# A new front, a batched shared expert and six folds inside the first routed stretch of a macaron block

## The reference

```python
router_logits = x @ gate_w                       # 16 experts
scores = sigmoid(router_logits)
_, selected = top_k(scores + expert_bias, 2)
top_scores = scores[selected] / (sum + 1e-20)
shared = silu(x @ shared_gate_w) * (x @ shared_up_w) @ shared_down_w
for e in range(E):                               # F = 128
    g, u = split(x @ experts_gate_up[e])
    routed += comb[:, e:e+1] * (silu(g) * u @ experts_down[e])
ffn = shared + routed

Q, K, V = x Wq^T, x Wk^T, x Wv^T                 # 3 heads of 256
attn = mean over heads of softmax(Q K^T / 16, over the query axis) V
out = attn @ fc_w.T + fc_b
```

## Time and profile before

| | us |
|---|---|
| median of 3 runs | 603.43 |
| lowest and highest | 601.87, 606.74 |
| the profiled execution | 605.9 |
| its span, first to last instruction | 604.7 |

### The profile page before, as it was taken

How to read it: one execution, slowest core, us unless ns; L and a number is a source line. 1 busy time by engine, 2 the same in 40 slices (tenths; PEclk the granted TensorE clock), 3 DMA queues, 4 the chain that set the end, 5 groups by cost and what they waited for, 6 DMA issues and landing times.

```text
span 604.7 us, 10587 instructions
## 1 busy us (share of the span) xinstructions
PE 478.6 (79%) x3212; PEld 434.0 (72%) x3212; DVE 366.6 (61%) x1118; ACT 274.9 (45%) x771; POOL 270.1 (45%) x278
## 2 busy tenths in 40 slices
PE   3632389999886799799899988999675899999600
PEld 3632389999774598699879977999563799998500
DVE  5567477566566366557645865543637776766543
ACT  3451147677541444354435443456241277776200
POOL 4654536566042163255226522422203566660675
PEclk9999999999998899899989999999955599999755
DMA  8661134667762010011001100010110156677455
GB/s 277 202 210 34 53 106 150 180 189 147 177 199 70 5 48 2 0 36 54 18 1 41 48 19 2 0 36 1 36 61 10 34 149 177 184 164 177 125 159 142
DMA packets 41077, 56.29 MB, mean 93 GB/s; under 512 B 6272, under 2 KB 33792, under 8 KB 41024
## 3 DMA queue, kind: packets, MB, share of 16 engines
q1 hardware_dynamic: 33024, 34.88, 17.8%
q0 software_dynamic: 7584, 20.72, 15.0%
q10 hardware_dynamic: 416, 0.02, 0.0%
HBM read 36.99 MB, written 18.61 MB: 92 GB/s over the span
## 4 chain that ended last, share of the span: by engine, by line
PE 59%; DVE 14%; DMA 12%; issue 5%; ACT 5%; POOL 5%; SPq 0%; POOLq 0%; ACTq 0%; DVEq 0%
PE bank L299 47%; PE bank L305 6%; DMA stage<-y_dram,slot_i 5%; DMA raw<-xn_dram,gather_at 2%; PE bank L432 2%; DMA raw<-xn_dram 2%; DVE x_sb L991 1%; PE bank L334 1%; POOL stage L1217 1%; DVE softmax_row L1114 1%; POOL w_lo L1167 1%; PE bank L389 1%; DVE x_sb L957 1%; DVE xn L817 1%; DMA xn_dram<-xn 1%
## 5 line engine op out<-in xcount | busy, mean ns | idle before, releaser
L299 PE MATMUL bank<-w_hi,xT 128*128 (+1 forms) x504 | 128.6, 317 | 0.0
L1323 POOL TENSOR_TENSOR e_sp<-raw,e_sp 128x512 fp32r<-128x512 f32 x48 | 62.5, 1302 | 134.7 <-ACT e_sp L773 134.6
L1246 POOL DMA_INDIRECT raw<-xn_dram,gather_at x94 | 89.3, 950 | 57.7 <-PE bank L305 46.8
L299 PEld LDWEIGHTS bank<-w_hi,xT 128*128 128x128 f32 x504 | 92.7, 202 | 0.3
L1217 POOL DMA_INDIRECT stage<-y_dram,slot_i x64 | 61.2, 957 | 51.8 <-issue 26.4
L299 PEld LDWEIGHTS bank<-v_sp,e_sp 128*128 128x128 f32 x576 | 75.8, 194 | 4.0 <-POOL e_sp L1323 1.1
L299 PE MATMUL bank<-v_sp,e_sp 128*128 128x256 f32 x576 | 78.0, 286 | 0.9 <-POOL e_sp L1323 0.9
L299 PE MATMUL bank<-g_sp,xT 128*128 128x512 f32 x288 | 75.2, 396 | 1.4 <-DVE g_sp L1022 1.4
L299 PE MATMUL bank<-w_lo,xT 128*128 (+1 forms) x252 | 74.2, 294 | 0.0
L299 PE MATMUL bank<-w_hi,e_sp 128*128 (+1 forms) x252 | 71.3, 303 | 2.0 <-DVE x_sb L1015 1.8
L305 PE MATMUL bank<-ident,raw 128*128 128x128 f32 x292 | 62.4, 298 | 8.8 <-DMA raw<-xn_dram 5.5
(11 more groups left out here) (112 smaller groups left out, 892.1 us busy)
## 6 DMA issues: line engine op xcount, KB each, us to landing
y_dram<-stage SPq DMA_DIRECT2D x94, 128.0 KB
raw<-xn_dram SPq DMA_DIRECT2D x32, 128.0 KB, 2.3
stage<-in_w_pack SPq DMA_DIRECT2D x9, 384.0 KB, 3.5
raw<-in_w_pack SPq DMA_DIRECT2D x8, 384.0 KB, 3.7
xn_dram<-raw SPq DMA_DIRECT2D x20, 128.0 KB, 1.7
x_sb<-in_x SPq DMA_DIRECT2D x4, 512.0 KB, 5.6
out<-x_sb SPq DMA_DIRECT2D x16, 128.0 KB, 2.3
raw<-xn_dram,gather_at POOLq DMA_INDIRECT x94, 3.4
```

What stands on the lines that cost most here:

```text
L299: m = pe.matmul(dst, lhs[k][l], rhs[k][r], start=(first and k == 0 and i == 0), stop=(last and k == n - 1 and i == 2), skip_group_check=True)
L1246: pool.indirect_dma_start(row_buf[:, n % ROWS, :], None, xn_dram, bass.IndirectOffsetOnAxis(ap=gather_at[:, j:j + 1], axis=0)).then_inc(s_ ...
L1323: pool.tensor_tensor(e_sp[:, i, 1, :], e32[:, i, :], e_sp[:, i, 0, :].bitcast(F32), ALU.subtract).then_inc(s_e_lo, 1)
```

## The change

**Front.** `STAGES` becomes 6. x is normalised by ScalarE into `xn_all`, which holds all 16 tiles; the scale and shift come from three small POOL instructions and a power. Tiles are turned in pairs into one bank, split into two parts for all 512 tokens of a batch (`front_x`), and the router uses three passes with a split gate. A whole batch is stored with one DMA. `xn_all` and a part of `front_x` lie where the folded weights lie later, and the new weight buffers where `e_sp` and `v_sp` lie.

**Shared expert.** It is taken out of the stretch, whose loop now has only the 47 slot tiles. It is made per batch: gate and up with 12 matmuls of 512 tokens (`shared_gu`), silu, product and two parts at 512 wide, and `shared_y` with 12 matmuls of 256. In the first FFN batches 0 to 2 are made beside the routing and batch 3 behind the stretch; in the second all four are made beside the routing.

**Index.** The picks are made in four chunks of eight pairs with no ring: one lane instruction a pair, and two wide instructions for all the tiles of a chunk.

**Folds.** All six are made in the first stretch, at steps 6, 13, 20, 27, 34 and 41 (`FOLD_STEPS`).

**Second front.** The normalised rows of batches 0 to 2, made beside attention and stored, are loaded back (`reload_batch`) and turned again; two pairs are turned ahead of attention's last mix.

```diff
-    EARLY = 8
-    STAGES = 4
-    FOLD_EVERY = 24
-    items = ([(SHARED, t) for t in range(EARLY)] + [(SLOT, j) for j in range(SLOT_TILES)]
-             + [(SHARED, t) for t in range(EARLY, NT)])
-    NI = len(items)
+    CHUNK = 8
+    EARLY_SHARED = 3
+    STAGES = 6
+    FOLD_STEPS = (6, 13, 20, 27, 34, 41)
+    NI = SLOT_TILES
...
@@ TensorE
+            def front_turn(r, n):
...
+                if n >= 2:
+                    pe.wait_ge(s_pair_lo, r * FRONT_PAIRS + n - 1)
...
+                for q in range(2):
+                    for k in range(KH):
+                        m = pe.transpose(bank[n % 2][:, k * PAIR + q * P:k * PAIR + (q + 1) * P],
+                                         xn_all[:, 2 * n + q, k * P:(k + 1) * P], ident[:])
+            def shared_gu(r, b):
...
+                for half, done in ((0, s_sg), (1, s_su)):
...
+                    three_pass(bank[shared_banks(b)[half]][:], lhs, rhs).then_inc(done, 1)
+            def shared_y(r, b):
+                pe.wait_ge(s_slo, c + 1)
...
+                    m = three_pass(bank[q // 2][:, q % 2 * H:(q % 2 + 1) * H],
+                                   [[shared_hT[:, part, q * P:(q + 1) * P] for part in range(2)]],
+                                   [[w_hi[:, at:at + H], w_lo[:, at:at + H]]])
...
+            for n in range(FRONT_PAIRS + 1):
+                if n < FRONT_PAIRS:
+                    front_turn(0, n)
+                if n > 0:
+                    front_router(0, n - 1)
+            shared_gu(0, 0)
+            shared_gu(0, 1)
+            rank_tokens(0)
+            shared_y(0, 0)
+            shared_gu(0, 2)
+            pack_experts(0)
+            shared_y(0, 1)
+            index_tokens(0)
+            shared_y(0, 2)
+            def between1(s):
+                if s in FOLD_STEPS:
+                    fold(next(folded))
+            ffn(0, between1)
+            shared_gu(0, 3)
+            shared_y(0, 3)
...
+            for w in MIXED_LATER:
+                if w == U - 1:
+                    front_turn(1, 0)
+                    front_turn(1, 1)
                 mix(w)
+            for n in range(2, FRONT_PAIRS - BATCH_PAIRS):
+                front_turn(1, n)
+            shared_gu(1, 0)
+            shared_gu(1, 1)
+            for n in range(FRONT_PAIRS - BATCH_PAIRS, FRONT_PAIRS):
+                front_turn(1, n)
+            for n in range(FRONT_PAIRS - BATCH_PAIRS, FRONT_PAIRS):
+                front_router(1, n)
+            rank_tokens(1)
+            shared_y(1, 0)
+            shared_gu(1, 2)
+            pack_experts(1)
+            shared_y(1, 1)
+            shared_gu(1, 3)
+            index_tokens(1)
+            shared_y(1, 2)
+            shared_y(1, 3)
+            ffn(1, lambda s: None)
...
@@ ScalarE, first front
+            front_norm(0, 0)
+            front_norm(0, 1)
+            front_hi(0, 0)
+            split_weight(0)
+            front_hi(0, 1)
+            front_norm(0, 2)
+            front_hi(0, 2)
+            split_weight(1)
...
+            run(choose(0, 0, NT))
+            shared_silu(0, 0)
+            shared_silu(0, 1)
+            for n in range(4, 8):
+                split_weight(n)
+            shared_hi(0, 0)
+            for n in range(8, 11):
+                split_weight(n)
+            shared_silu(0, 2)
+            shared_hi(0, 1)
+            for n in range(11, 14):
+                split_weight(n)
+            shared_hi(0, 2)
+            for n in range(14, NW):
+                split_weight(n)
...
@@ VectorE, the picks in routing
+                for c in range(len(pairs_of) // CHUNK):
+                    for n in range(c * CHUNK, (c + 1) * CHUNK):
+                        if n % 4 != 1:
+                            dve.tensor_scalar(pick_lane[:, n, :], lane_no[:], lane_i[:, k, t:t + 1], None,
+                                              ALU.is_equal).then_inc(s_lane_dve, 1)
...
+                    chained(dve.tensor_tensor(
...
+                    dve.tensor_tensor(pick_tile[:, t0:t1], pick_tile[:, t0:t1],
+                                      token_no[:, t0:t1].unsqueeze(2).unsqueeze(3).to_broadcast(shape),
+                                      ALU.mult).then_inc(s_pick_tile, 1)
...
-                dve.wait_ge(s_inv, (r + 1) * len(pairs_of))
+                dve.wait_ge(s_inv, r + 1)
                 dve.tensor_copy(gather_at[:], index).then_inc(s_indexed, 1)
...
@@ VectorE, first front after choose
+            shared_mul(0, 0)
+            shared_mul(0, 1)
+            r1 = routing(0)
+            next(r1)
+            next(r1)
+            shared_lo(0, 0)
+            next(r1)
+            next(r1)
+            next(r1)
+            split_weight(5)
+            next(r1)
+            shared_sink(0, 0)
+            shared_mul(0, 2)
+            next(r1)
+            shared_lo(0, 1)
+            next(r1)
+            split_weight(8)
+            next(r1)
+            shared_sink(0, 1)
+            split_weight(11)
+            shared_lo(0, 2)
+            split_weight(14)
+            shared_sink(0, 2)
+            run(r1)
...
@@ VectorE, second front after choose
+            shared_mul(1, 0)
+            shared_mul(1, 1)
+            r2 = routing(1)
...
+            shared_lo(1, 0)
...
+            shared_sink(1, 0)
+            shared_mul(1, 2)
+            shared_lo(1, 1)
...
+            shared_sink(1, 1)
+            next(r2)
+            shared_mul(1, 3)
+            shared_lo(1, 2)
+            shared_sink(1, 2)
+            shared_lo(1, 3)
+            shared_sink(1, 3)
+            run(r2)
...
@@ POOL, first front
+            for b in range(B):
+                front_rstd(0, b)
+            for n in range(NW):
+                if n % 3 != 2:
+                    split_weight(n)
+                    if n == 12:
+                        lanes(0)
...
@@ SP, first front
             for n in range(STAGES):
                 load_weight(n)
+            for b in range(B):
+                store_batch(0, b)
+            for n in range(STAGES, NW):
+                load_weight(n)
+            load_fold(0)
```

More of the change, by code:

```diff
@@ L186, in macaron @@
         fcb_sb = route[:, 6, 0:H]
-        stages = [buf[:, i * WCOLS:(i + 1) * WCOLS] for buf in (stage, raw) for i in range(2)]
+        stages = [buf[:, i * WCOLS:(i + 1) * WCOLS] for buf in (stage, raw, stage_more) for i in range(2)]
         fold_in = route[:, 0:4, :].rearrange("p (m k) h -> p m k h", m=2)
@@ L728, in act_program @@
-            next(r1)
-            splits = iter(range(NW))
-            for n in range(50):
-                if NW * (n + 1) // 50 > NW * n // 50:
-                    split_weight(next(splits))
-                next(r1)
-            attn_side = [attn_front(b) for b in range(B)]
+            act.wait_ge(s_zeroed, 1)
+            act.activation(score[:, 0, 0:1], minus_half[:, 0:1], ACT.Sigmoid).then_inc(s_warm, 1)
+            act.wait_ge(s_small, 32)
+            act.copy(gate_sp[:, 0], gate_raw[:]).then_inc(s_gate_hi, 1)
@@ L749, in act_program @@
+            shared_hi(0, 3)
+            attn_side = [attn_front(b) for b in range(B)]
             run(attn_side[0])
@@ L1379, in choose @@
                 for _ in range(4 + 2 * (n // 4)):
-                    yield
-            def routing():
-                for _ in range(4 + len(pairs_of) // GROUP + 1 + 2):
                     yield
```

863 lines of the change are left out of this document (409 added, 454 removed).

## The result

The changed kernel took 615.7 us (median of four runs, 614.8 to 616.7), the kernel before, run beside it, 604.0: ratio 1.019, 95% interval 1.015 to 1.024. It is slower. The forecast was 605, no change, with 599 to 611 as its own range; 615.7 lies outside that and inside the whole range of 588 to 618, near its slow end. The profiled execution's span (first to last instruction) is 615.1 us, where it was 604.7.

What follows compares the result with a forecast made beforehand. Routing, weights and index were taken to bound the first front, TensorE the first routed stretch. Terms -16.0 + 2.5 + 11.2 - 3.2 + 5.5 + 1.5 = +1.5 gave 605 us, no change; range 588 to 618, its own 599 to 611.

Steps and rivals of the forecast that it cites:

- the first front: Start to slot 0: the new order brings slot 0 to 71.8 instead of 87.8, -16.0 us (-22 to -10).
- the second rival: Both fronts: VectorE's chain bounds, POOL blocks in full, weights slide; +15, 618 us; chance 0.30 together with the third.
- the last three-pass router: First front, after ScalarE's last copy at 22.7: lower half and 12 small matmuls, done at 25.3.
- the GpSimd block: First front: POOL's weight splits hold up VectorE's counting, up to 7 us or nothing; 2.6 taken.
- Folds and fill: First routed stretch: four more folds at 2.8 us, +11.2, and filling the pipeline, +2.5 (1 to 4).
- Last product to attention: After the first stretch: the fold ahead of attention's turns is gone, -3.2 us (-1 to -5); shared batch 3 hidden.
- Second front: Before the second stretch: shared batches and sinks ahead of the index move slot 0 by +5.5 us (-1 to +11).
- rival 4: Both fronts: index ready early, copied late behind sinks; copied at once, 4 us each, 597; chance 0.34 with another rival.
- The granted clock: Second front: taken as 0.54; far over that was named as a sign of the prediction being wrong.
- Second stretch: Slot 0 to first result gather: filling costs +2.5, 1 comes back without shared rows loaded; +1.5 us (0 to 4).
- The third: First stretch: the folds' loads collide with gathers, 16 instead of 11.2, 610 us; chance 0.30 together with the second rival.

Runs made afterwards that it cites:

- stacked router: Changed kernel with early weight splits, early index copy and the first front's router products in 8 instead of 12 matmuls a pair: 603.1 us, on another chip 591.8 us.
- the kernel that only waits: Changed kernel with GpSimd's fourth low part of a weight waiting until VectorE has counted, all else the same: 626.1 us, ratio 1.004.

## Where the prediction held and where it failed, step by step

The result lies in the stated range, but not by the mechanism of the forecast: the first front failed by 16.1 us, and smaller errors of the other sign, 8 us together, brought the sum back within 11. The range reached to 618 for the sake of the second rival; that 615.7 fell inside it was partly luck.

**The first front, -16.0 and in fact +0.1: this is the step that failed,** and with it the forecast. Its own working gives two errors, which the runs confirm one by one.

1. "ScalarE has ... 1.7 us, eight pairs 13.6, last copy at 22.7", then "the last three-pass router": the router's matmuls were counted for the last pair alone, as if TensorE did the others beside ScalarE's work. They are TensorE's own pace: 12 matmuls at 0.215, which is 2.6, and the turns make 3.33 a pair in steady state. 8 x (3.33 - 1.7) is 13.0 of the 13.5 us by which the router was late (38.8 against 25.3). With one product instead of three a pair took 1.6 to 2.4 us, 1.9 in the mean, and the router ended at 27.5. Forgetting them cost so much because TensorE stood at its low level: at the second front's 0.119 a matmul and 8 turns in 1.03 us, a pair would be some 1.9 us (an estimate from these rows), and the router late by 2. The price stood in the trace of the kernel before, whose first front has the same small matmuls:

```profile
12.06 0.87 PE L334 MATMUL bank<-gate_raw,route 128*128 128x16 f32 x4
```

2. "I take 2.6" for the GpSimd block: the upper bound of 7 was the right end. Count to the last step of the slots took 11.9 us in the changed kernel and 5.3 where GpSimd waited, 6.6 us. Three more instructions between 74.5 and 81.8 took 4.8 us more than their shapes do elsewhere (2.52, 2.29 and 2.57 against 0.95, 0.68 and 0.95), a second meeting that the prediction didn't have. The rest of the chain was some 3 us shorter than counted, so ranks to index was 35.8 us, not 27.8 and 2.6. The Trainium skill, SBUF — State Buffer, section "Who interferes with whom", has the shared port pair as an exclusive lock, for which a VectorE instruction with two SBUF inputs contends with a GpSimd instruction that reads SBUF. The trace agrees: 5.46 us against 0.80 for the same four additions. I had cited the rule and weighed it by one cast of 1.09 us, which had met GpSimd only in part.

Together they are the 16.3 us by which the index was late (82.9 for 66.6, the 64.0 and the 2.6 for the block): the router 13.5, less 2.6 for the shared batches and ranks behind it, which took 8.3 us where I had 10.9, and 5.4 for the chain (35.8 for 30.4). The index's way to slot 0 was 4.9 for 5.2.

**Folds and fill, +13.7 and in fact +9.8.** The fold was 2.56 for 2.8, its number right; four make 10.2. The fill cost +3.0 (slots 0 to 5 turned within 10.0 us, where five plain steps make 7.0), for 2.5. What I had not subtracted is that 51 plain steps at 1.40 and two folds made 77 us of the old 81.0: the old stretch held another 4 us, the new one 1.0 (90.8 less 71.4 of steps, 15.4 of folds and 3.0 of fill). The trace of the kernel before shows where most of it lay. From slot 42 on its turns lost 2.3 us to late rows, 1.33 of them in one wait:

```profile
161.55 0.44 PE L305 MATMUL bank<-ident,raw 128*128 128x128 f32 x2 [1.33 <-DMA raw<-xn_dram,gather_at]
```

And from the turn of the last slot to the last product it took 7.2 us, where the new stretch, which turns nothing more there, took 6.5. Why the rows were late was not tried.

**Last product to attention, -3.2 and in fact -3.3.** Right in size; the reason given, that the fold ahead of the turns is gone, fits the rows and was not tested alone. That shared batch 3 hides there holds too: taking it away brought attention 0.3 us nearer to the gather.

**Second front, +5.5 and in fact +3.9.** Ranks to index 26.8 us, in the 25 to 28 given. The index was late behind the sinks, as rival 4 said, but copying it at once is worth 2 to 4 us in this front, not 4 in each: in the first it is worth nothing, where the last low parts then release slot 0, and 1.6 once the weights are early. In the changed kernel itself the index did release slot 0, as said, but by 2 us only: the last low parts ended at 80.9 and 81.8. The granted clock was 0.83, not near 0.54. I had named that as a sign of being wrong; this front's term held all the same.

**Second stretch, +1.5 and in fact -1.0.** Outside its bounds of 0 to 4 by 1 us. The fill came, but smaller (slots 0 to 5 turned within 8.2 us, 1.2 over plain steps, for 2.5). The rest is again time of the old stretch over plain steps: there the last slot's turn to the first result gather took 11.2 us, here 9.4.

**The rivals.** The second one happened, by its own test: slot 0 after 76 in the first front and after 489 in the second. Its mechanism, the block in full with the weights sliding, is part of the failed term; it lacked the router. Its 618 is 2 us from the result, the forecast 11, but its terms are not the measured ones (first front -10 for +0.1, second front +10 for +3.9, its fill +3 for -1.0), so the nearness is luck. The third, loads of the folds colliding with gathers, 16 instead of 11.2, didn't happen: four folds cost 10.2, and with three of the six outside the stretch the time stayed at 616.7. With the router counted for every pair at 3.33 the sum would have been 605 + 13.0, and slower the likeliest case. That this is near 615.7 owes something to chance too: the 5.4 missing for the block and 8 us too much in the other terms would still have stood in it.

## What to carry to other kernels

A pipelined loop over tiles has a pace on each engine, so write down for each engine all that it does for one tile and take the largest; a term that stands in the sum "for the last one" is often the pace of all. Where two engines hold each other up, as VectorE and GpSimd did here (four additions 5.46 us beside the low parts, 0.80 without), ask which of one's long instructions will stand beside the other's short chained ones after a reordering. Put them where the other waits; here a wait alone only moved the bill. A block of fixed work (a fold) cost its time in the stretch, which TensorE paced, and as much behind it, where it waited for its own matrices; in a gap that another engine made it cost little (1 us at most for the fold at 53.5): look for the gap before choosing the step.

## What the runs showed of the hardware that was not expected

**The granted clock read 1.00 while TensorE's pace was that of 1.2 GHz.** A window of the changed kernel inside the router, and one of the kernel before:

```profile
16.00:36.00 20.00, 20.00 (x98) 20.00 (x97) 4.92 (x7) 7.68 (x13) 6.26 (x5) 1.00 0.33 112
...
70.00:78.00 8.00, 5.14 (x29) 4.21 (x29) 4.56 (x21) 2.58 (x5) 2.66 (x5) 1.00 0.11 33
```

From 16 to 36 TensorE is busy throughout and the column reads 1.00, the 2.4 GHz level. Yet the 512-column matmuls that begin at 38.65 start every 0.42 us, which is 1.2 GHz, until 42.15, and from there every 0.23, the 2.4 GHz level, as the rows of PE above show. The 16-column matmuls before them went at 0.215 each, those of the second front at 0.119. In the kernel before the column reads 1.00 for the whole first front, while 256-column matmuls at 78.7 to 81.7 started every 0.21 us, as at the low level in the earlier trace rows. So the column can't be trusted in the first front of these profiles, and 1.00 before against 0.84 after tells nothing; the pace of rows of one shape can be trusted.

**A matmul of 32 columns cost the same 0.215 us as one of 16.** PE of the stacked router:

```profile
16.02 0.59 PE L365 MATMUL bank<-gate_sp,xT 128*128 128x32 f32 x2
16.45 0.57 PE L368 MATMUL bank<-gate_sp,xT 128*128 128x16 f32 x2
```

Two of either take 0.43 us from start to start; the 16 further columns were free. Each has its own 128x128 weight load, and these stand back to back too (12 in 2.68 us in the changed kernel's PEld rows at 16.83). That they set the pace is argued, not tested.

**One chip slowed some kernels more than others.** The kernel before was 3.5% slower on the second chip (623.8 against 602.8), the one with stacked router 1.9% (603.1 against 591.8). In the profiles from it the second stretch took 82.7 to 85.2 us instead of 76.0 to 78.2, at a granted clock that was no lower (0.95 in the kernel that only waits against 0.94 in the changed one, 0.99 against 0.99 in the one with stacked router). Why is open; it was not tried.
